# Folding the coupling row's affine step from VectorE into the broadcast matmul and the ScalarE write, with a new wait ahead of the epilogue's transposes

## What is computed

```python
gf = _global_net(x.mean(axis=1, keepdims=True), gc_w1, gc_b1, ..., gc_b3)
out = x
for _ in range(3):
    h = _gelu(out @ cn_w1 + cn_b1)          # 1024 -> 1024
    h = _gelu(h @ cn_w2 + cn_b2)            # -> 512
    h = _gelu(h @ cn_w3 + cn_b3)            # -> 256
    tf = jax.nn.sigmoid(h @ cn_w4 + cn_b4)  # -> 1, one number per token
    coupling = 0.1 + adaptive_range * (0.7 * gf + 0.3 * tf - 0.5) * 2.0
    out = out + coupling * _twist(out)      # quarters: [p_r, -p_i, -o_r, o_i]
return out
```

## Time and profile before

| | us |
|---|---|
| median of the runs (3403.07 and 3408.06) | 3405.56 |
| the profiled execution | 3411.7 |
| span of its slowest core (core 7) | 3410.2 |
| spans of the eight cores | 3387.6 to 3410.2 |
| PE busy / DVE busy / ACT busy | 2157.2 / 1353.2 / 1149.5 |

### The profile page before, as it was taken

One profiled execution on the slowest core, in us unless ns is written; L12 is line 12 of the kernel. 1 busy time (PEld: TensorE's weight loads), 2 busy tenths in 40 slices (PEclk: granted clock), 3 DMA queues, 4 the chain that ended last, 5 costly groups with the idle time before them and its releaser, 6 DMA issues. The chain is left out here.

```text
span 3410.2 us, 35577 instructions; the slowest of 8 cores (3387.6 to 3410.2 us)
## 1 busy us (share of the span) xinstructions
PE 2157.2 (63%) x10736; PEld 1050.9 (31%) x10736; DVE 1353.2 (40%) x2041; ACT 1149.5 (34%) x1840; POOL 40.7 (1%) x71
## 2 busy tenths in 40 slices
PE   0468687777552857575706786878774527675666
PEld 0122223131110545454502232222311115454444
DVE  1063545545342333433311636364553413334334
ACT  0126171716200333333301453627170013333333
POOL 1000000000000000000000000000000000000000
PEclk9978787887786878687857786868687868786777
DMA  7410100000212010100071101000002110100000
GB/s 113 66 33 5 22 1 1 1 13 1 50 49 40 1 38 4 34 7 32 1 126 33 29 1 22 1 1 1 13 1 62 50 28 5 33 9 30 12 26 25
DMA packets 111651, 87.02 MB, mean 26 GB/s; under 512 B 84592, under 2 KB 89200, under 8 KB 111472
## 3 DMA queue, kind: packets, MB, share of 16 engines
q0 software_dynamic: 20336, 34.36, 6.7%
q1 hardware_dynamic: 91136, 50.40, 5.1%
HBM read 85.47 MB, written 16.78 MB: 30 GB/s over the span
## 5 line engine op out<-in xcount | busy, mean ns | idle before, releaser
L1158 PE MATMUL pBIG<-outTbf,cw1sb 128*128 128x256 bf16 x3072 | 466.2, 326 | 42.0 <-ACT h1T L1171 41.8
L673 DVE TENSOR_TENSOR prdsb<-pexpsb,vtsb 128x1024 bf16<-128x1024 bf16 x512 | 354.0, 692 | 303.5 <-ACT pexpsb L658 269.1
L1158 PEld LDWEIGHTS pBIG<-outTbf,cw1sb 128*128 128x128 bf16 x3072 | 342.9, 116 | 178.2 <-issue 70.0
L658 ACT ACTIVATE pexpsb<-pBIG 128x1024 bf16<-128x1024 f32 x344 | 344.4, 1022 | 64.8 <-PE pBIG L644 55.3
L546 PE MATMUL pBIG<-prodb,indt 128*32 128x512 bf16 x1024 | 228.3, 536 | 152.0 <-DVE prodb L520 127.0
L459 PE MATMUL pQK<-x0T,wqsb 128*128 128x512 bf16 x512 | 130.1, 422 | 236.6 <-DMA x0T<-x0tok 236.6
L644 PE MATMUL pBIG<-pfm,expf 128*128 128x512 bf16 x688 | 230.6, 422 | 73.0 <-ACT pexpsb L658 59.0
L1171 ACT ACTIVATE h1T<-pBIG,cb1sb 128x256 bf16<-128x256 f32 x384 | 181.5, 474 | 262.1 <-PE pBIG L1158 261.9
L511 DVE COPY kr<-ktsb 64x512 bf16<-64x512 bf16 x128 | 36.5, 285 | 449.4 <-ACT ktsb L472 447.4
L1191 PE MATMUL pQK<-h1T,cw2sb 128*128 128x256 bf16 x1536 | 175.5, 272 | 42.2 <-ACT h1T L1171 42.2
L520 DVE TENSOR_TENSOR prodb<-qtsb,kr 128x2048 bf16<-128x2048 bf16 x128 | 156.9, 1226 | 100.2 <-PE pBIG L546 91.9
(11 more groups left out here) (176 smaller groups left out, 2120.7 us busy)
## 6 DMA issues: line engine op xcount, KB each, us to landing
x0f<-x SPq DMA_DIRECT2D x32, 512.0 KB, 3.6
out<-x2slab SPq DMA_DIRECT2D x32, 512.0 KB, 2.6
x0tok<-x POOLq DMA_DIRECT2D x32, 256.0 KB, 3.9
x0T<-x0tok SPq DMA_TRANSPOSE x256, 2.3
wqsb<-wqT POOLq DMA_DIRECT2D x2, 2048.0 KB, 18.3
wksb<-wkT POOLq DMA_DIRECT2D x2, 2048.0 KB, 29.9
wvsb<-wvT POOLq DMA_DIRECT2D x2, 2048.0 KB, 41.5
wfcsb<-wfcT POOLq DMA_DIRECT2D x2, 2048.0 KB, 17.2
```

The lines of the kernel that those rows point to most:

```text
L658: a.activation(pexpsb[:, slot * 1024: slot * 1024 + 1024], pvb, AF.Copy).then_inc(s_pev.h, 1)
L673: v.tensor_tensor(bass.AP(prdsb, slot * 1024, [[2048, 128], [512, 2], [1, 512]]), bass.AP(pexpsb, slot * 1024, [[2048, 128], [512, 2], [1, ...
L1158: mm = te.matmul(SLOT[bank][:, 0:256], cw1sb[:, (k * 8 + dch) * 128: (k * 8 + dch) * 128 + 128], outTbf[:, k * 512 + hf * 256: k * 512 + h ...
```

## The change

The affine step A + B * t no longer runs on DVE. B goes into the weights of the broadcast matmul, A into the bias of ScalarE's write:

- In the global network, `dv12` also computes -A (`abrow[3]`) and a row of 128 times B, which it puts into `lnb` (the attention's buffer for logarithms, free at that time). `pe11` and the copy behind it spread four numbers over the partitions (`ccols`) and not three.
- `dvc4` is gone, and `peB` multiplies `tanhrow` with the B row. It waits for ACT (`s_h`) and no longer for DVE (`s_tw`).
- `acC4` uses Identity with a bias column (A, or -A beside the scale of -1) in place of Copy.
- The first `peU` of each tile also waits for the last updates of both halves (`twA`, `twB`, the semaphore values of the two `dvU`). Before, the wait of `peB` for DVE covered the first half's, since DVE runs in order.

```diff
             v.drain()
+            v.tensor_scalar(abrow[0:1, 3:4], abrow[0:1, 0:1], -1.0, None, ALU.mult)
+            v.tensor_scalar(lnb[0:1, 0:128], onesf[0:1, :], abrow[0:1, 1:2], None, ALU.mult)
+            v.drain()
             nc.vector.engine_nop().then_inc(s_gc.h, 1)
...
-            te.matmul(pR[:, 30:31], onesf[0:1, :], abrow[0:1, 2:3],
+            te.matmul(pR[:, 30:32], onesf[0:1, :], abrow[0:1, 2:4],
...
-            v.tensor_copy(ccols[:, 2:3], pR[:, 30:31]),
+            v.tensor_copy(ccols[:, 2:4], pR[:, 30:32]),
...
-                    def dvc4(v, th_t=th_t):
-                        v.wait_ge(s_h.h, th_t)
-                        v.tensor_scalar(c4row[0:1, :], tanhrow[0:1, :],
-                                        abrow[0:1, 1:2], abrow[0:1, 0:1],
-                                        ALU.mult, ALU.add)
-                        v.drain()
-                        nc.vector.engine_nop().then_inc(s_tw.h, 1)
-                    P.dve.append(dvc4)
-                    c4_t = s_tw.inc()
-
-                    def peB(te, c4_t=c4_t):
-                        te.wait_ge(s_tw.h, c4_t)
-                        te.matmul(pA[:, 0:256], onesf[0:1, :], c4row[0:1, :],
+                    def peB(te, th_t=th_t):
+                        te.wait_ge(s_h.h, th_t)
+                        te.matmul(pA[:, 0:256], lnb[0:1, 0:128], tanhrow[0:1, :],
...
-                        a.activation(C4N[:, 256:512], pA[:, 0:256], AF.Copy)
+                        a.activation(C4N[:, 256:512], pA[:, 0:256], AF.Identity,
+                                     bias=ccols[:, 0:1])
...
-                                     AF.Copy, scale=-1.0).then_inc(s_h.h, 1)
+                                     AF.Identity, scale=-1.0,
+                                     bias=ccols[:, 3:4]).then_inc(s_h.h, 1)
...
-                        ebank=ep_bank[0]):
+                        ebank=ep_bank[0],
+                        twA=cast_ready_h[0], twB=cast_ready_h[1]):
                     if ep_first:
                         te.wait_ge(s_h.h, tfree)
+                        te.wait_ge(s_tw.h, twA)
+                        te.wait_ge(s_tw.h, twB)
```

## The result

The changed kernel takes 3373.16 us (median of 19 runs, 3366.28 to 3430.52); the kernel before took 3407.52 in the 18 runs beside them. The ratio is 0.9894, with a 95% interval of 0.9866 to 0.9922: 36 us faster by the ratio, 34.4 by the medians, where 21.5 was forecast. In single executions of either kernel the cores of one die show a lower granted clock and take longer; the ratios leave these out, so medians of scattered runs are read here with their lowest run. The profiled execution took 3366.3 us (span 3364.7, core 1; the eight cores 3351.8 to 3364.7).

The account below looks back on a forecast made before the run. PE, waiting behind DVE's step between tanh and the broadcast matmul, was taken to bound the feed-forward half-cycle; -17.0 - 5.1 - 6.2 + 6.0 + 0.8 = -21.5 us on 3405.56 gave 3384.1 us, range 3368 to 3400.

Parts of the forecast that it names:

- The hop, 34 x 0.50: In 34 ordinary half-cycles the broadcast matmul, waiting directly for ACT, starts 0.50 us earlier: 17.0 us gained (13.6 to 21.8).
- The bias: ACT's two C4N writes with a bias column cost 0.09 us more each, 0.18 per half, hidden in ordinary halves.
- The clock, 0.15 per half: In ordinary halves an earlier broadcast matmul more often meets the higher PE clock level: 0.15 us per half, 5.1 us gained.
- The bound of 36 us: Most the clock could gain: broadcast matmul and layer 1 as the cheapest case in all 34 halves, 34 x 1.06.
- "cheapest" 9.54: Shortest profiled PE time for broadcast matmul and layer 1 together, 9.54 us, against a mean of 10.60.
- a seventh of the way: The clock's gain was taken as a seventh of the distance from mean to cheapest layer 1: 0.15 us per half.
- Boundaries, 6 x 1.04: At six tile boundaries the first sumtile addition comes 1.04 us earlier, despite late transposes: 6.2 us gained (0 to 18).
- Last halves, 2 x 3.0: At each batch's end the transposes wait for both updates, so the sumtile addition comes 3.0 us later: 6.0 us lost.
- 0.8: Global-context step, twice per core: two more DVE operations and a drain before pe11, 0.8 us lost (0.5 to 1.1).
- The first: Rival: layer 1 runs longer at the lower clock level and gives the 0.50 back; 3406 us, chance 0.10.
- The third: Rival: Identity is missing from ACT's loaded table, so each half reloads twice; 3439 to 3507 us, chance 0.03.
- The second: Rival: the clock adds to the gain, layer 1 always as the cheapest; 52.4 us gained, 3353 us, chance 0.06.

Follow-up runs that it names:

- The kernels with 0.83, 1.21 and 1.81: Changed kernel with a DVE stop put back in 36 half-cycles: without operation, with 32 columns, with two operations; 3384.02, 3405.06, 3424.97 and 3496.05 us.
- the fillers: Changed kernel with unused extra matmuls in PE's gaps: 4 behind layer 4, median 3351.37 us; also 5 behind each of layers 1 to 3, 3300.14 us.

## Why the prediction was right, and where it was too small

The time, 3373.16, lies in the range of 3368 to 3400 and within 2%, 11 us below the forecast of 3384.1. It lies near the range's lower end: the ratio of 0.9894 on 3405.56 is 3369.5, with 3359.9 to 3379.0 as its interval, so a little luck was needed to stay inside. By the prediction's own steps:

- **The hop, 34 x 0.50.** Right in mechanism: PE waits 0.71 in every half and all of it is on the path. Off in size: I took the hand-over from ACT to PE as 0.25, from the matmul behind h3T; behind tanh it is 0.15, so the hop is worth 0.60, and 34 x 0.60 = 20.4 us for 17.0, inside the bounds. Why the hand-over behind h3T is the longer one isn't known.
- **The bias.** Right: 474 for 384 ns and 680 for 591, hidden.
- **The clock, 0.15 per half.** This is the term that was mis-sized. D fell by 11.41 - 10.96 = 0.45, 34 x 0.45 = 15.3 us where I had 5.1; the broadcasts already at the lower level went from 38 to 22 of 48. The mechanism was named (an earlier matmul meets the higher level more often), but "a little more often" was a third of all halves. "The gap's length matters little" was drawn from boundary halves at 5.7, and it is nearly true above 1.3 us and says nothing of below: both lie where D hardly answers any more. It also rested on one row (10.59). Over all cores of the kernel before, broadcast matmul and layer 1 took 10.70 at boundaries and 10.50 in ordinary halves, and at boundaries every broadcast ran at the lower level. The kernels with 0.83, 1.21 and 1.81 show where it flattens, and the fillers show the other end. The bound of 36 us for the term held, though single halves went below its "cheapest" 9.54 (7.93); inside it I chose the value nearest to the mean, with no row that spoke for a seventh of the way.
- **Boundaries, 6 x 1.04.** Right in mechanism (Ptw behind the cast, the addition behind the evacuation, idle for 2.12) and in size: from the last cast to the addition the mean fell from 10.61 to 9.55, by 1.06. The boundary column fell by 0.64 only, so 3.8 us for 6.2, because the last cast itself comes 0.42 later behind layer 2 (35.81 for 35.39). Nearly all of that lies inside SP's chain, which takes 36.57 us from its start to the last cast and not 36.18; the prediction had it unchanged, and its cause stays open.
- **Last halves, 2 x 3.0.** "Last" rose by 2.38; it holds one ordinary hop and one D, worth 1.05 together, so the term itself is 3.43, and 6.9 us for 6.0. DVE's idle stretch is 3.52, as predicted.
- **Sum by these steps:** -20.4 - 15.3 - 3.8 + 6.9 + 0.8 = -31.8, for 34.4 measured.
- **Rivals.** The first, that the clock gives the gain back, falls: D went down. The third falls with the 6 table loads that stayed. The second, layer 1 always as the cheapest, came true in part: 15 us of its 36 in this change, and more than all of it (D from 11.41 to 8.83) once PE is filled. It had a chance of 0.06, too little for a mechanism whose size no row of before bounded tightly.

The Trainium skill (ScalarE: Activation LUTs, "Table sets: the hidden batching unit") put the third rival at nil, and the trace agrees: 6 loads at the return to Gelu before and after, 18 in all in both. The Trainium skill (TensorE: Matmul & The Clock Gate, "A second HAM failure mode: psum-queue depth-cycling") tells of a kernel in which short idle moments between groups of matmuls made the clock swing between its levels and cost throughput; this case agrees, with idle pieces of 0.7 to 1.3 us and D from 8.83 to 11.41.

## What to carry to other kernels

Before a short idle piece on PE is priced at its length, look whether the granted clock falls around it, and take the mean over all cores and halves, not one row: here 0.60 us less of idleness was worth 1.05, and useless matmuls in the idle pieces were worth over three times the whole hop (73 against 20 us). A flat response between two long gaps is no evidence about short ones. And where a wait is added to a step that reads its inputs in parts, wait for each part at the step that reads it: that alone gave 13.7 us here.

## What was not expected of the hardware

The cost of the lowered clock hardly grows with the gap beyond a point: it is there almost fully at 1.2 us of idleness (D34 11.29) and little larger at 1.31 and 1.81 (11.39 and 11.47), while at 0.71 and 0.83 it is 0.4 to 0.5 lower and varies from half to half (7.93, 9.60 or 10.88 us for the same matmuls). With 0.16 us before the broadcast and the other pieces filled too, D is 8.83, and 8.59 to 9.11 in single half-cycles. ACT's end to PE's start behind a single semaphore was 0.15 us; a bare pass through DVE's queue added 0.12 us to the gap (0.83 against 0.71), and so DVE's operation and drain make up 0.48 of the 0.60; with 32 columns in place of 256 they still make up 0.38. Idle waits of PE with the same name can be worth quite different amounts: 5.4 us at a boundary bought 1.4, and 0.60 in an ordinary half bought 1.05.
